# First attention: band mask matmuls left out of the scores, and GpSimd selects that zero the exponentials outside the band

## The reference, cut to what matters

```python
scores = jnp.einsum('bqhd,bkhd->bhqk', q, k) / jnp.sqrt(d)        # 16 batches, 8 heads, 512 x 512
band = jnp.abs(idx[:, None] - idx[None, :]) <= local_size         # local_size = 64
scores = jnp.where(band[None, None], scores, neg)
attn = jax.nn.softmax(scores, axis=-1)
o = jnp.einsum('bhqk,bkhd->bqhd', attn, v)
```

## Time and profile before

| | us |
|---|---|
| three runs of the kernel | 1461.33, 1466.27, 1466.6 |
| median | 1466.27 |
| span of the profiled execution (first to last instruction) | 1463.7 |
| PE / DVE / ACT / POOL busy in it | 1354.5 / 1002.8 / 791.5 / 249.2 |
| exponentials of the first attention (L383), first start to last start | 45.5 to 477.3 |

### The profile page before, as it was taken

One profiled execution on the slowest core, in us unless ns is written; L12 is line 12 of the kernel. 1 busy time (PEld: TensorE's weight loads), 2 busy tenths in 40 slices (PEclk: granted clock), 3 DMA queues, 4 the chain that ended last, 5 costly groups with the idle time before them and its releaser, 6 DMA issues. The chain is left out here.

```text
span 1463.7 us, 28639 instructions
## 1 busy us (share of the span) xinstructions
PE 1354.5 (93%) x8666; PEld 813.1 (56%) x8666; DVE 1002.8 (69%) x3234; ACT 791.5 (54%) x1802; POOL 249.2 (17%) x265
## 2 busy tenths in 40 slices
PE   3678999999999799999989999999789999999998
PEld 1345555555555444444455555555434777777774
DVE  8889999999997646456546788887659654545211
ACT  4777888888888733332357677776530233332331
POOL 4100000000000100000010000002411255555552
PEclk7699999999999999999999999999999999999999
DMA  8534344343440300000020000000322588888885
GB/s 261 145 87 99 91 107 106 86 119 90 107 104 17 145 1 0 0 0 0 0 75 15 16 16 14 14 1 2 146 85 93 184 247 251 255 257 246 255 233 115
DMA packets 63186, 149.52 MB, mean 102 GB/s; under 512 B 10792, under 2 KB 27830, under 8 KB 58892
## 3 DMA queue, kind: packets, MB, share of 16 engines
q1 hardware_dynamic: 49836, 115.70, 26.1%
q0 software_dynamic: 13280, 32.93, 9.6%
HBM read 113.21 MB, written 35.39 MB: 102 GB/s over the span
## 5 line engine op out<-in xcount | busy, mean ns | idle before, releaser
L776 DVE CUSTOM_DVE_ANT_0 masked_scores<-ps_max,band_mask 128x192 bf16<-128x192 f32 (+1 forms) x512 | 177.2, 383 | 20.5 <-PE ps_max L505 13.9
L383 ACT ACTIVATE probs_t<-ps_sc 128x448 f32<-128x448 f32 x256 | 138.7, 542 | 80.4 <-PE ps_sc L525 78.1
L1255 PE MATMUL f_ps<-f_xt,w_t 128*128 (+1 forms) x704 | 160.2, 382 | 2.5 <-ACT w_t L1310 2.5
L377 ACT ACTIVATE nf_above<-nf_scaled,nf_sign_at 128x512 f16<-128x512 bf16 x231 | 161.5, 715 | 0.0
L2803 DVE TENSOR_TENSOR d_inter<-d_silu_g,d_su 128x384 f32<-128x384 f32 x32 | 17.7, 554 | 159.6 <-PE d_su L2487 154.4
L1927 ACT ACTIVATE c_probs<-d_sg,c_negmax 128x128 f32<-128x128 f32 x256 | 90.3, 365 | 58.1 <-DVE c_negmax L2012 57.7
L1255 PEld LDWEIGHTS f_ps<-f_xt,w_t 128*128 128x128 bf16 x704 | 69.3, 98 | 86.7 <-issue 5.0
L2320 POOL DMA_INDIRECT out<-d_h,d_scatter_now x64 | 97.2, 1519 | 108.3 <-DMA out<-d_h,d_scatter_now 92.9
L505 PE MATMUL ps_max<-k_stack,q_stack 96*128 96x192 bf16 (+1 forms) x512 | 96.5, 272 | 19.8 <-DVE row_max L776 13.8
L2671 DVE TENSOR_SCALAR d_onehot<-d_slot_no,d_pos 128x192 bf16<-128x192 bf16 x512 | 101.0, 288 | 0.3 <-PE d_lb L2388 0.3
L505 PEld LDWEIGHTS ps_max<-k_stack,q_stack 96*128 96x128 bf16 x512 | 46.2, 101 | 92.1 <-issue 46.9
(11 more groups left out here) (381 smaller groups left out, 2830.1 us busy)
## 6 DMA issues: line engine op xcount, KB each, us to landing
d_wgu<-in_ex_gu SPq DMA_DIRECT2D x32, 1024.0 KB
d_wdown<-in_ex_d SPq DMA_DIRECT2D x32, 512.0 KB
dr_parts<-qk_parts SPq DMA_DIRECT2D x32, 384.0 KB, 4.8
q_stack<-dr_parts SPq DMA_DIRECT2D x32, 192.0 KB, 2.7
k_stack<-dr_parts SPq DMA_DIRECT2D x32, 192.0 KB, 3.3
out<-x_sb SPq DMA_DIRECT2D x21, 256.0 KB, 2.2
nf_w<-in_nf_w POOLq DMA_DIRECT2D x3, 1408.0 KB, 10.2
q_stack<-dr_parts SPq DMA_DIRECT2D x32, 128.0 KB, 2.4
```

Source lines behind the costliest of these rows:

```text
L377: act.activation(above[:, g, k, :], lvl[:, g, :], ACT.Sign, bias=cut[:, k - NDV:k - NDV + 1]).then_inc(s_sg, 1)
L383: act.activation(pt[:, c, :], SP[c % 2][:].rearrange("p a w -> p (a w)")[:, a:z], ACT.Exp, scale=D0 ** -0.5).then_inc(s_e, 1)
L776: op = dve.tensor_tensor_reduce(masked[:, c % 2, k, off:off + hi - lo], M[c % 2][:, k, off:off + hi - lo], mask[:, k, off:off + hi - lo], ...
L1255: mm = pe.matmul(bank[:], w12[:, m, kt, ft * P:(ft + 1) * P], xt[:, q, kt, bass.ds(g * N, N)], start=(kt == 0 and q == 0), stop=(kt == KT ...
```

## The change

The mask matmul goes out of `scores`, and each of the two score matmuls now starts its own accumulation. ACT computes the exponential of all 448 columns unmasked. GpSimd then runs two affine selects a chunk on `probs_t`, each over 2 x 128 columns (the lower and the upper edge of the band), that keep the value inside the band and put 0.0 outside. `pv` waits for these (`s_in`) in place of the exponentials. `probs_t` grows from 448 to 512 columns a chunk so that both halves have the same shape; two memsets zero the columns that no exponential writes. The POOL program thus gets the loop over the batches, with `spread_scales` and `gather_maxima` at fixed places in it.

```diff
-    pt = sb("probs_t", [P, 8, 2 * WIN - BAND], F32)
+    pt = sb("probs_t", [P, 8, 2, WIN], F32)
...
-            pool.wait_ge(s_sc, 1)
-            spread_scales(0, 1)
-            pool.wait_ge(s_am, 5)
-            gather_maxima(1, 3)
-            pool.wait_ge(s_sc, 2)
-            spread_scales(1, 3)
+
+            def band(u, c):
+
+                pool.wait_ge(s_e, 8 * u + c + 1)
+                pool.nop(nofuse=True)
+                low, high = pt[:, c, :, 0:P], pt[:, c, :, P:WIN]
+                pool.affine_select(out=low, in_=low, compare_op=ALU.is_ge, fill=0.0, base=0,
+                                   pattern=[[0, 2], [1, P]], channel_multiplier=-1)
+                pool.affine_select(out=high, in_=high, compare_op=ALU.is_ge, fill=0.0, base=0,
+                                   pattern=[[0, 2], [-1, P]], channel_multiplier=1).then_inc(s_in, 1)
+
+            def body(j, i, b, first, last, final):
+                for c in range(8):
+                    band(2 * i, c)
+                if first:
+                    pool.wait_ge(s_sc, 1)
+                    spread_scales(0, 1)
+                for c in range(8):
+                    band(2 * i + 1, c)
+                    if c == 4 and isinstance(i, int) and i == 1:
+                        pool.wait_ge(s_sc, 2)
+                        spread_scales(1, 3)
+                if first:
+                    pool.wait_ge(s_am, 5)
+                    gather_maxima(1, 3)
...
                 s = SP[c % 2]
-                a, z = kept(kp)
-                pe.matmul(s[:].rearrange("p a w -> p (a w)")[:, a:z], identb[:],
-                          mask[:].rearrange("p a w -> p (a w)")[:, a:z], start=True, stop=False)
                 for k in range(2):
                     kt = 2 * kp + k
                     lo, hi, off = chunk_cols(kt)
                     mm = pe.matmul(s[:, k, off:off + hi - lo], kst[0:98, b, h, kt * P:(kt + 1) * P],
-                                   qst[0:98, b, h, lo:hi], start=False, stop=(k == 1))
+                                   qst[0:98, b, h, lo:hi], start=True, stop=True)
                 mm.then_inc(s_s, 1)
 
             def pv(u, b, g, kp):
-                pe.wait_ge(s_e, 8 * u + 4 * kp + 4)
+                pe.wait_ge(s_in, 8 * u + 4 * kp + 4)
```

More of the change, by code:

```diff
@@ L174, in phase_layer0_attention @@
     s_s, s_e, s_pv = sem("a_scores"), sem("a_exp"), sem("a_pv")
+    s_in, s_pad = sem("a_probs_in_band"), sem("a_probs_pad")
     s_oc, s_oT, s_rs, s_on = sem("a_o_copy"), sem("a_o_turn"), sem("a_o_recip"), sem("a_o_norm")
@@ L336, in _ @@
             load_nf(2)
-            pool.wait_ge(s_sc, 1)
-            spread_scales(0, 1)
-            pool.wait_ge(s_am, 5)
-            gather_maxima(1, 3)
-            pool.wait_ge(s_sc, 2)
-            spread_scales(1, 3)
+            def band(u, c):
[20 more added lines that the diff above has]
+                    gather_maxima(1, 3)
+            pool.wait_ge(s_ko, 1)
+            pool.memset(pt[:, 0:4, 0, 0:BAND], 0.0).then_inc(s_pad, 1)
+            pool.wait_ge(s_pad, 1)
+            pool.memset(pt[:, 4:8, 1, WIN - BAND:WIN], 0.0).then_inc(s_pad, 1)
+            pool.wait_ge(s_pad, 2)
+            batches(pool, body)
         @block.scalar
@@ L382, in exps @@
                 a, z = kept(c // 4)
-                act.activation(pt[:, c, :], SP[c % 2][:].rearrange("p a w -> p (a w)")[:, a:z], ACT.Exp, scale=D0 ** -0.5).then_inc(s_e, 1)
+                act.activation(pt[:, c].rearrange("p a w -> p (a w)")[:, a:z], SP[c % 2][:].rearrange("p a w -> p (a w)")[:, a:z], ACT.Exp, scale=D0 ** -0.5).then_inc(s_e, 1)
             def o_copy(u, g):
@@ L537, in pv @@
                         mm = pe.matmul(O[32 * j:32 * j + 32, lo:hi], va[:, b, kt, 4 * g + j, :],
-                                       pt[:, 4 * kp + j, k * WIN + off - kept(kp)[0]:k * WIN + off - kept(kp)[0] + hi - lo],
+                                       pt[:, 4 * kp + j, k, off:off + hi - lo],
                                        start=(kt == 0), stop=(kt == QT - 1), skip_group_check=True)
```

## The result

| | before | changed |
|---|---|---|
| median, us | 1466.43 (1461.33 to 1466.97, 4 runs) | 1482.15 (1479.1 to 1485.87, 4 runs) |
| ratio | | 1.0118, 95% interval 1.0098 to 1.0138 |
| span of the profiled execution | 1463.7 | 1479.0 |

The change makes the kernel 1.2% slower. In a second measurement beside other kernels the ratio was 1.0122 (1.01 to 1.0144).

What follows compares the result with a forecast made beforehand. The prediction took DVE to bound the steady stretch, with slack on PE: span 1463.7 - 12 (gain) + 30 (compares) + 3 (wait on GpSimd) = 1485, stated as 1486 us; range 1456 to 1513, likeliest case 1474 to 1510.

Steps and rivals of the forecast that it cites:

- So DVE bounds this stretch, and PE has slack.: Steady batches, 62 to 435 us: DVE busy 351.92 of 373 us, waiting 11.7 us for PE, so DVE sets the pace.
- Gain, 12 us.: Without the mask matmul DVE waits less for PE: 9 us in the steady stretch, 3 in first and last batches.
- PE's granted clock, taken at nothing: PE's clock, 0.98 in the steady stretch, could fall with less PE work; costed at nothing, since PE has slack.
- "half-clocked" first batches: First batches at half clock, where exponentials follow scores more directly; with the last batch they add 3 us of gain.
- Loss of the compares, 30 us.: DVE's SBUF-to-SBUF compares wait behind selects: 132 pairs, six of eight met, 0.3 us each; range 10 to 50 us.
- Operations with two SBUF inputs, nothing taken, bound 18 us.: Some 90 DVE operations with two SBUF inputs were taken to lose nothing beside selects; at the other end 18 us.
- The maxima's operations spared.: DVE's 512 maxima operations, with PSUM and one SBUF input, lose nothing beside selects; the 256-column one stays at 417 ns.
- The wait on GpSimd, 3 us.: 2 us for selects queued behind scale transfers in batches 0 and 1, 1 us for the last value product.
- The slack that I gave as 1.6 us: Value products waiting for selects cost PE nothing as long as GpSimd isn't over 1.6 us late.
- POOL busy by some 200 us more.: Sign in the changed profile: two selects a chunk, 0.39 us each, over 256 chunks make 200 us of POOL busy.
- "DVE is the bound, so these count in full.": The compares' waits behind selects, 30 us (10 to 50), all lengthen the program, because DVE bounds it.

Runs made afterwards that it cites:

- e3: Kernel before, plus the same selects after each exponential on a side tile that nothing else uses, so no engine waits for them: 1475.44 us, ratio 1.008.
- e6: Kernel before, mask matmul kept, with the third bf16 part of queries and keys computed by GpSimd in place of DVE: 1462.25 us, ratio 0.9981.
- e7: Kernel before with both the third bf16 part of queries and keys and the gate product moved from DVE to GpSimd: 1464.94 us, ratio 1.0004.
- e1: Changed kernel without its selects, so no mask matmul and nothing zeroed outside the band: 1459.28 us, ratio 0.997 to the kernel before.
- e5: Changed kernel with GpSimd's wait inside batch 0's scale gather moved three select pairs later: 1480.94 us, ratio 1.0118 to the kernel before.
- e4: Kernel before, plus memsets of the same shape as the selects, after each exponential, on an otherwise unused side tile: 1467.47 us, ratio 1.0027.
- e2: Changed kernel with the mask matmul back, so both mask matmul and selects: 1478.05 us, ratio 1.0107 to the kernel before.
- e9: Changed kernel with each pair of selects waiting for the next chunk's exponential: 1507.83 us, ratio 1.0289 to the kernel before.
- e10: Changed kernel with the mask matmul back and each select pair waiting for the next chunk's exponential: 1517.78 us, ratio 1.0369 to the kernel before.
- e11: Half the change: selects replace the mask matmul only in chunks 4 to 7, chunks 0 to 3 keep it: 1471.52 us, ratio 1.0045 to the kernel before.
- e12: The changed kernel measured and profiled once more, with no edit: 1480.73 us, ratio 1.0122 to the kernel before.

## Why the prediction was right, point by point

The forecast was 1486 us, the measurement 1482.15, and the direction and the mechanism hold: DVE stands still behind GpSimd's selects, and this outweighs PE's relief. Two terms were too large, of opposite sign, and one left at zero was not zero. So the mechanism was foreseen, and that the number is only 4 us off is luck in part.

- **"So DVE bounds this stretch, and PE has slack."** Half right. A longer DVE makes the batch longer (e3), but DVE's margin over PE is 1.5 us in 235 (e6, e7). I read DVE's share of 94% as a bound with slack behind it; the waits of the earlier trace rows point both ways, and I took the larger for the truth. For a loss this did no harm. Had the change been one that relieves DVE, the same reading would have promised too much, as my expectation for e6 did, by 6 to 12 us.
- **Gain, 12 us.** Mis-sized: 4.4 us alone (e1; 6.0 between the medians). DVE's waits for PE, of which I took three quarters, fell hardly at all in the changed kernel. I had called the gain the part by which DVE stops waiting; in the nine batches of e1 DVE's idle time fell by 2.6 us, and its busy time by 2.4 too, though no kind of operation got shorter by over 2%. Busy time counts overlapping instructions once, so I take it that waits too short to show as idle time went as well.
- **PE's granted clock, taken at nothing, and "half-clocked" first batches.** The clock was 0.82 and 0.90 in batches 0 and 1 before, and 0.76 in both of the changed kernel. From 62 to 435 us it fell from 0.98 to 0.96. Its price isn't shown (e5).
- **Loss of the compares, 30 us.** Mis-sized: 12.4 us by their mean (281 to 328 ns, where I wrote some 400). I counted six of eight pairs met, at 0.3 us each. The count was right: in the nine batches 59 of 72 pairs lie beside a select. The price was not: such a pair takes 0.58 us from its start to its end and another 0.48, so it is 0.1 us, the low end of my range. Most pairs beside a select don't wait, since 27 compares have all of the stall, 0.2 us each.
- **Operations with two SBUF inputs, nothing taken, bound 18 us.** Wrong to leave at zero: 7.8 us by their means (8.2 with the nine scalings of another form). The earlier trace rows showed such a sum unharmed inside a POOL operation, and I gave that more weight than the rule of the Trainium skill; e3 against e4 shows the rule true for the selects. Against the loss of 30, which was 18 too much, this is 8 too little, and the gain was some 7 too much: the errors partly cancel.
- **The maxima's operations spared.** Right: 417 ns.
- **The wait on GpSimd, 3 us.** About right in size: e2 less e3 is 2.6 us in the medians, with overlapping intervals. In the nine batches there is no such price (239.71 and 240.19 us); 2.2 us of it lie ahead of them (131.4 and 129.2 up to the 65th exponential). The slack that I gave as 1.6 us exists, some 1.3 by e9, which shows what happens when it goes.
- **POOL busy by some 200 us more.** It was 237 us on the page (249.2 to 486.7), since selects wait for DVE as well.
- **"DVE is the bound, so these count in full."** True only of the kernel without the mask matmul: from e1 to the changed kernel the nine batches grow by the 10.5 us of the stalls, and less the 5.0 of the relief this is the 5.5 measured. With the mask matmul kept about half of the stalls counts (e2, e3, e4). So gain and loss are not independent: with the selects there, leaving the mask out takes 0.9 us in nine batches instead of giving 5.0. DVE's stalls grow by 2.7 us, since the selects fall elsewhere against its work: the float16 sums (1234 to 1319 ns) and the gates (680 to 833) now wait longer behind one, and the third parts (774 to 682) no more. Where they fall is read from the traces. That the earlier scores move them is my explanation: e9 and e10, meant to test it, changed the slack too.

## What to carry to other kernels

Before work goes to an idle GpSimd, list what DVE does at those moments from SBUF alone: TENSOR_SCALARs between SBUF tiles and operations with two SBUF inputs stand still behind GpSimd, those that read PSUM and one SBUF tile don't. An idle engine is then not free. Whoever starts second stands, so the same work can cost DVE nothing where it starts second: in e11 half as many selects cost DVE nothing in the nine batches. And when two engines are each over 90% busy, relieving either may be worth no more than the distance to the other, and slowing one may cost less than the stall: measure that distance by taking work away from each in turn before counting on it.

## What the runs showed of the hardware that I had not expected

- GpSimd's operations in a row can leave DVE no turn: one compare of 0.28 us took 2.42 us while seven selects followed each other 0.36 us apart (once, in one of two profiles of the changed kernel).
- GpSimd's subtraction of 512 float32 columns took 1.17 us here. The compares kept 282 ns in e6, the float16 sum was held up by it (1213 to 1440 ns).
- PE stood still for 3 us just behind the loop in e11's profile, of which the profile names only "issue"; in the same place of eight others (before, changed, e1, e2, e3, e9, e10, e12) its waits of this kind sum to at most 1.4 us. Comparisons of whole programs at the grain of 0.3% include such pieces, comparisons of the steady loop do not.
